# A graph layer on one core: the first three groups fed from six shared edge chunks, and the search for the others by differences of rows

## What is computed

```python
msg = jax.nn.relu(x[src] + edge_attr)
agg = jax.ops.segment_sum(msg, dst, num_segments=50000)
h = x + agg
h = jax.nn.relu(h @ W1 + b1) @ W2 + b2
out = layernorm(x + jax.nn.relu(h), axis=-1)
```

## Time and profile before

| | us |
|---|---|
| median of 3 runs | 477.14 (476.47 to 477.19) |
| the profiled execution | 474.89 |
| its span, first to last instruction | 473.0 |
| PE busy | 457.9 (97%) |
| DVE busy | 434.3 (92%) |
| ACT busy | 395.7 (84%) |
| POOL busy | 365.7 (77%) |

### The profile page before, as it was taken

One profiled execution on the slowest core, in us unless ns is written; L12 is line 12 of the kernel. 1 busy time (PEld: TensorE's weight loads), 2 busy tenths in 40 slices (PEclk: granted clock), 3 DMA queues, 4 the chain that ended last, 5 costly groups with the idle time before them and its releaser, 6 DMA issues.

```text
span 473.0 us, 10533 instructions
## 1 busy us (share of the span) xinstructions
PE 457.9 (97%) x3033; PEld 378.0 (80%) x3033; DVE 434.3 (92%) x1761; ACT 395.7 (84%) x924; POOL 365.7 (77%) x403
## 2 busy tenths in 40 slices
PE   7879999999999999999999999999999999999994
PEld 5657888888888888888888888888888888888883
DVE  5658999999999999999999999999999999999996
ACT  2349888888888989888988888888889898888885
POOL 6546888888877776787888888888888888888843
PEclk9989999999999999999999999999999999999998
DMA  5625666666667676666666666666666666666632
GB/s 131 178 75 174 185 197 192 197 194 196 195 179 208 180 207 182 209 180 195 192 199 191 196 196 193 199 190 196 194 196 190 200 187 202 186 198 188 198 110 87
DMA packets 83613, 86.80 MB, mean 184 GB/s; under 512 B 11767, under 2 KB 79252, under 8 KB 83556
## 3 DMA queue, kind: packets, MB, share of 16 engines
q1 hardware_dynamic: 74388, 68.76, 46.3%
q0 software_dynamic: 8496, 17.38, 14.2%
q10 hardware_dynamic: 672, 0.00, 0.1%
HBM read 60.51 MB, written 25.60 MB: 182 GB/s over the span
## 4 chain that ended last, share of the span: by engine, by line
PE 95%; DVE 1%; another core or an unknown queue 1%; ACT 1%; issue 0%; DMA 0%; DVEq 0%
PE h_ps L930 37%; PE h1T_ps L922 36%; PE hT_ps L886 12%; PE hT_ps L859 9%; PE h1T_ps L413 1%; DMA dst_first<-in_dst_dram 0%; ACT h1T L777 0%; PE prep_ps L423 0%; ACT hT L771 0%; DVE h L632 0%; DVE stats L653 0%; ACT std L782 0%; DVE z L646 0%; PE prep_ps L912 0%
## 5 line engine op out<-in xcount | busy, mean ns | idle before, releaser
L115 POOL DMA_INDIRECT x_src<-in_x_dram,src_of x256 | 269.4, 1052 | 84.8 <-issue 58.0
L930 PE MATMUL h_ps<-w_sb,h1T 128*128 128x128 f32 x1564 | 197.9, 276 | 1.8 <-issue 1.6
L922 PE MATMUL h1T_ps<-hT,w_sb 128*128 128x384 f32 (+1 forms) x524 | 191.6, 488 | 3.7 <-ACT hT L771 3.7
L777 ACT ACTIVATE h1T<-h1T_ps,b_sb 128x384 f32<-128x384 f32 (+1 forms) x262 | 151.7, 580 | 50.7 <-issue 32.7
L930 PEld LDWEIGHTS h_ps<-w_sb,h1T 128*128 128x128 f32 x1564 | 185.5, 192 | 2.6 <-issue 2.1
L922 PEld LDWEIGHTS h1T_ps<-hT,w_sb 128*128 128x128 f32 x524 | 89.9, 192 | 39.0 <-ACT hT L771 3.5
L796 ACT ACTIVATE y<-z,shift,rstd 128x128 f32<-128x128 f32 x261 | 113.6, 482 | 0.6 <-DVE shift L673 0.5
L632 DVE TENSOR_TENSOR h<-h_ps,b_sb 128x384 f32<-128x384 f32 x131 | 72.7, 555 | 25.6 <-PE h_ps L930 14.7
L549 POOL TENSOR_SCALAR y<-z,rstd,shift 128x128 f32<-128x128 f32 x123 | 85.1, 692 | 13.6 <-DVE shift L673 9.1
L653 DVE BATCH_NORM_STATS2 stats<-z 128x6 f32<-128x128 f32 x391 | 88.7, 282 | 0.1
L859 PEld LDWEIGHTS hT_ps<-ident,x_sb 128*128 128x128 f32 (+1 forms) x379 | 49.5, 142 | 39.6 <-issue 22.8
(11 more groups left out here) (133 smaller groups left out, 182.8 us busy)
## 6 DMA issues: line engine op xcount, KB each, us to landing
x_sb<-in_x_dram SPq DMA_DIRECT2D x130, 192.0 KB
out_dram<-y SPq DMA_DIRECT2D x130, 192.0 KB
pre_msg<-in_edge_attr_dram SPq DMA_DIRECT2D x130, 128.0 KB
x_src<-in_x_dram,src_of POOLq DMA_INDIRECT x256
w_sb<-in_w_dram SPq DMA_DIRECT2D x2, 128.0 KB
dst_rows<-in_dst_dram SPq DMA_DIRECT2D x1, 97.7 KB
x_src<-in_x_dram,first_pairs POOLq DMA_INDIRECT x4, 2.7
b_sb<-in_b_dram SPq DMA_DIRECT2D x1, 64.0 KB, 3.1
```

The source lines that it names most:

```text
L115: nc.gpsimd.indirect_dma_start(out=c["x_src"][:, g % EB, k, :], out_offset=None, in_=x, in_offset=bass.IndirectOffsetOnAxis(ap=index, axis ...
L777: nc.scalar.activation(h1T[:, h, 0:n, 0:p], h1T_ps[h][:, 0:n, 0:p], ACT.Relu, bias=b1_sb[:, h:h + 1]).then_inc(h1_ready, 1)
L922: nc.tensor.matmul(h1T_ps[h][:, 0:n, 0:p], w1_sb[:, h * 128:(h + 1) * 128], hT[:, 0:n, 0:p], start=True, stop=True).then_inc(h1_summed, 1)
L930: last = nc.tensor.matmul(h2_ps[g % 2][0:p, t, :], h1T[:, h, t, 0:p], w2_sb[:, h, :], start=(h == 0 and t == 0), stop=(h == HC - 1), skip_ ...
```

## The change

Three things.

1. **Groups 0 to 2 from fixed chunks.** Six chunks of 128 edges (edges 0 to 767) serve the first three groups together. `FIRST_SELS` lists nine pairs of group and chunk, with the range of columns that the pair can reach; a chunk that straddles two groups is multiplied once for each. The search begins at group 3 (`FIRST_ROW = 3`). `msg_whole` is gone: every chunk has a high and a low part.
2. **The search by differences.** Instead of marking the one row that holds a boundary, DVE marks all rows before it (`row_before`), and PE multiplies with `row_steps`, the difference of each row to the row before it, so that the sum telescopes to the wanted row. This drops `dst_next`, `next_of` and `row_holds`, and needs a second copy of the list, moved by one row (`dst_prev`, 99 KB), and one subtraction of 125x200. ACT's conversion of the rows (L403) is gone.
3. **The checks moved** from the first groups to groups 8 to 26 of the steady loop; PE's part (`find_ends`) to group 10. The steps of the search on DVE after the counting are interleaved with the first messages.

The orders of the first groups on all five engines are written anew. Core of the diff:

```diff
-FIRST_ROW = 2
+FIRST_ROW = 3
-TARGETS_FOUND, TARGETS_CHECKED, CHECKED = (12, 16), 20, 30
+ENDS_MARKED, ENDS_FOUND, ENDS_CHECKED = 8, 10, 12
+ORDER_FOUND, ORDER_CHECKED, LIMITS_CHECKED = 14, 16, 18
+TARGETS_FOUND, TARGETS_CHECKED, CHECKED = (20, 22), 26, 30
-FIRST_CHUNKS = 4
-PARTS = {g: [slice(0, 1), slice(1, 2)] for g in range(4)}
+FIRST_GROUPS, FIRST_CHUNKS = 3, 6
+FIRST_SELS = [(0, 0, 0, 128), (0, 1, 56, 128),
+              (1, 1, 0, 92), (1, 2, 0, 128), (1, 3, 72, 128),
+              (2, 2, 0, 56), (2, 3, 0, 128), (2, 4, 16, 128), (2, 5, 88, 128)]
+PARTS = {g: [slice(0, 1), slice(1, 2)] for g in range(FIRST_GROUPS)}
...
# sync
+        start_edge_attr(sp, edge_attr, 2, 2 * K * EW, c)
         sp.wait_ge(c["window_loaded"], 16)
+        start_x(sp, x, 2, 2, c)
...
-        load_ea(2)
-        load_x(2)
         load_ea(3)
         load_x(3)
...
# gpsimd, first part
+        for k in range(2):
+            pool.wait_ge(pairs_loaded[k], 16)
+            start_first_gather(nc, x, k, c)
+        pool.wait_ge(more_pairs_loaded, 16)
+        start_first_gather(nc, x, 2, c)
+        start_first_gather(nc, x, 3, c)
+        pool.wait_ge(start_ready, 1)
+        start_windows(nc, pairs, c)
+        start_first_gather(nc, x, 4, c)
+        start_first_gather(nc, x, 5, c)
...
# vector, search
-        link(dve, nc.vector.tensor_scalar(row_before[:, 0:K, :], node_row[0:ROWS, 0:K, :], first_of[:, 0:1], None, ALU.is_gt))
-        dve.wait_ge(next_loaded, 16)
-        link(dve, nc.vector.tensor_tensor(next_of[:, :], dst_next[:, :], highest[:, :], ALU.max))
...
+        dve.wait_ge(dst_loaded, 16)
+        dve.wait_ge(prev_loaded, 16)
+        dve.wait_ge(prev_cleared, 1)
+        nc.vector.tensor_tensor(row_steps[:, 1:ROW + 1], dst_rows[:, :], dst_prev[:, :], ALU.subtract).then_inc(row_steps_ready, 1)
+        dve.wait_ge(pool_consts, 5)
+        dve.wait_ge(first_dst_ready, 1)
         select_first(nc, 0, c)
         select_first(nc, 1, c)
...
# scalar, loads
+        for k in range(2):
+            act.dma_start(first_pairs[:, k, :], pairs[k * EW:(k + 1) * EW, :]).then_inc(pairs_loaded[k], 16)
+        act.dma_start(dst_prev[1:ROWS, :], dst[0:edges - ROW].rearrange("(r e) -> r e", e=ROW)).then_inc(prev_loaded, 16)
+        act.dma_start(first_pairs[:, 2:FIRST_CHUNKS, :], pairs[2 * EW:FIRST_CHUNKS * EW, :].rearrange("(k p) a -> p k a", p=EW),
...
# vector, first groups
+        checks["count_starts"](dve)
+        checks["first_edges"](dve)
         add_edge_attr(0, 0)
+        checks["split_edges"](dve)
+        dve.wait_ge(c["first_dst_ready"], 2)
+        select_first(nc, 2, c)
+        checks["start_edges"](dve)
+        low_part(0, 0)
         add_edge_attr(0, 1)
+        select_first(nc, 3, c)
+        low_part(0, 1)
         add_edge_attr(1, 0)
+        select_first(nc, 4, c)
         low_part(1, 0)
+        add_edge_attr(1, 1)
+        select_first(nc, 5, c)
+        low_part(1, 1)
+        select_first(nc, 6, c)
+        select_first(nc, 7, c)
+        add_edge_attr(2, 0)
+        select_first(nc, 8, c)
+        low_part(2, 0)
         target_nodes(nc, dve, dst_ps, c).then_inc(targets_ready, 1)
+        add_edge_attr(2, 1)
+        add_bias(0)
+        low_part(2, 1)
         dve.wait_ge(targets_ready, 1)
...
         select(3)
         add_x(0)
         statistics(0)
         aggregate(0)
+        add_edge_attr(3)
         add_bias(1)
+        low_part(3)
...
# scalar, first groups
         high_part(0, 0)
+        high_part(0, 1)
+        copy_hT(0)
+        high_part(1, 0)
+        hidden(0, 0)
+        high_part(1, 1)
         act.wait_ge(c["starts_summed"], 1)
...
+        hidden(0, 1)
+        high_part(2, 0)
+        copy_hT(1)
         source_nodes()
         hidden(1, 0)
+        high_part(2, 1)
         hidden(1, 1)
         copy_hT(2)
         hidden(2, 0)
+        deviation(0)
+        high_part(3)
         hidden(2, 1)
         copy_hT(3)
...
# tensor, first groups
+        sum_first(0, fill=True)
+        checks["keep_busy"](1, 256)
+        sum_first(1, final=True)
+        checks["turn_starts"](pe)
         turn_x(1)
+        sum_first(2)
         pe.wait_ge(c["w1_loaded"], 16 * (1 + HC))
         hidden_sum(0)
+        sum_first(3)
+        pe.wait_ge(c["w2_loaded"], 16)
+        output_sum(0, 0)
+        sum_first(4, final=True)
+        output_sum(0, 1)
         pe.wait_ge(c["starts_row_ready"], 1)
         turn_windows(nc, pe, src_ps, dst_ps, c)
+        hidden_sum(1)
+        turn_x(2)
+        for i in range(5, 8):
+            sum_first(i)
+        output_sum(1, 0)
+        sum_first(8, final=True)
+        output_sum(1, 1)
+        hidden_sum(2)
+        turn_x(3)
+        output_sum(2, 0)
+        sum_messages(3)
+        output_sum(2, 1)
...
+            if g == ENDS_FOUND:
+                checks["find_ends"](pe)
```

More of the change, by code:

```diff
@@ L70, in parts_to @@
     return sum(len(parts(i, c)) for i in range(g))
-def halves_to(g, c):
-    return sum(len(parts(i, c)) - (i in WHOLE) for i in range(g))
 def loads_to(slot, g):
@@ L83, in gathers_to @@
 def gathers_to(slot, g, c):
-    return 16 * sum(windows(i, c) for i in range(slot, g + 1, EB) if i >= 4)
+    return 16 * sum(windows(i, c) for i in range(slot, g + 1, EB) if i >= FIRST_GROUPS)
 def rows(dram, g, c):
@@ L427, in prepare_tensor, with keep_busy, turn_starts @@
                              start=(t == 0), stop=False, skip_group_check=True)
[L428 removed]
+        keep_busy(1, 256)
+    def keep_busy(times, columns):
+        for _ in range(times):
+            nc.tensor.matmul(c["h1T_ps"][0].rearrange("p t n -> p (t n)")[:, 0:columns], ident[:, :],
+                             ident[:, :] if columns == 128 else c["x_sb"][:, 0, 0:2, :].rearrange("p t d -> p (t d)"),
+                             start=True, stop=True)
+    def turn_starts(pe):
         pe.wait_ge(starts_ready, 1)
         nc.tensor.matmul(starts_ps, window_start[:, 0:1], ident[0:R, 0:R], start=True, stop=True).then_inc(starts_summed, 1)
[L431 removed]
     return dict(sync=prepare_sync, gpsimd=prepare_gpsimd, vector=prepare_vector, scalar=prepare_scalar, tensor=prepare_tensor,
[L434 removed]
+                keep_busy=keep_busy, turn_starts=turn_starts, count_starts=count_starts, first_edges=first_edges,
+                split_edges=split_edges, start_edges=start_edges, mark_ends=mark_ends, find_ends=find_ends, check_ends=check_ends,
+                find_order=find_order, check_order=check_order, check_limits=check_limits, find_targets=find_targets,
+                check_targets=check_targets, set_general=set_general, sum_flags=sum_flags)
 def main_path(nc, x, pairs, edge_attr, out, c, sb, sem, checks):
@@ L738, in main_vector @@
                 add_edge_attr(g + 3)
+            if g == ENDS_MARKED:
+                checks["mark_ends"](dve)
+            if g == ENDS_CHECKED:
+                checks["check_ends"](dve)
+            if g == ORDER_FOUND:
+                checks["find_order"](dve)
+            if g == ORDER_CHECKED:
+                checks["check_order"](dve)
+            if g == LIMITS_CHECKED:
+                checks["check_limits"](dve)
             if g in TARGETS_FOUND:
@@ L903, in sum_second @@
[L903 to L914 removed]
+            pe.wait_ge(msg_lo_ready, parts_to(g, c) + 1)
@@ new lines, in sum_messages @@
+            for k in range(windows(g, c)):
+                if g == LAST:
+                    p0, p1, tile = 0, LP, last_sel[:, :]
+                elif g == END:
+                    p0, p1 = (0, WP) if k == 0 else (END_LO, END_LO + END_WP)
+                    tile = end_sel[:, k, :]
+                else:
+                    p0, p1, tile = LO[k], LO[k] + WP, sel[:, g % EB, k, :]
+                cols = tile.rearrange("p (t q) -> p t q", t=n)[:, :, 0:p1 - p0]
+                for part in (msg_hi, msg_lo):
+                    last = nc.tensor.matmul(sum_bank(g)[:, 0:n, p0:p1], part[:, g % EB, k, :], cols,
+                                            start=False, stop=(k == windows(g, c) - 1), skip_group_check=True)
```

313 lines of the change are left out of this document (106 added, 207 removed).

## The result

The change made the kernel slower: 483.99 us (median of 4 runs, 483.25 to 485.17) against 477.16, a ratio of 1.0149 with a 95% interval of 1.0126 to 1.0171. The forecast was 474.5, its range ended at 477.5. The profiled run took 485.17, its span 483.5.

What follows compares the result with a forecast made beforehand. PE, busy 97% of the span, was taken as the bound, so only an earlier start of its series helps. Terms -1.0 - 1.2 - 0.9 + 0 + 0.35 + 0.2 = -2.55: 477.14 - 2.6 = 474.5 us, range 467.5 to 477.5.

Steps and rivals of the forecast that it cites:

- and land at 12.1: Search, at the start: POOL's windows go out at 8.7 and land at 12.1 instead of 11.73, not needed before 14.5.
- The loads: At the start: dst_prev lands at 4.8, PE begins the search 0.2 later, bounds 0.3 earlier to 1.0 later.
- Groups 0 and 1: First two groups: hidden_sum(0) at 11.2 instead of 12.23, -1.0 us; hidden_sum(1) at 15.0 instead of 17.18, -1.2 more.
- Groups 2 and 3: Next two groups: hidden_sum(2) at 18.8, hidden_sum(3) at 22.3 against 25.4 for before without its pause, -0.9 us more.
- with 3.2 us the second is there at 19.9: Group 3's second gather, started at 16.7, takes 3.2 us from issue to use and is there at 19.9.
- The checks in the series: Checks moved into the steady loop: PE's two matmuls in group 10 cost +0.35 us, DVE's pieces +0.2 (0 to 2.6).
- The pause: ACT's waits near 20 to 26 us for PE work long done, priced at 6.5 us; the change leaves it, 0.
- rival 1: At the start: the pause goes with something the new order avoids, gaining 6.5 us more, to 468.0; chance 0.31.
- The clock: PE's clock at the start: busy about 3.9 of 4.6 us from 10.4 to 15.0, so nothing charged.
- rival 2: PE falls to half clock between 9 and 23 us, 2.5 us a group; two groups give 479.5; chance 0.12.
- Rival 3: In the series: DVE can't hide the checks, PE pays 2.6 us instead of 0.2, giving 476.9; chance 0.11.
- The median: Whole run: the runs' median stands 2.25 us above the profiled execution, carried over to the forecast without a reason.

Runs made afterwards that it cites:

- e1: The changed kernel with FIRST_ROW back at 2, so 128 windows are searched and fetched instead of 127: 474.67 us, 0.994 of the kernel before.
- e3: e1 with seven more window gathers in the series, of 128, 127, 126, 120, 112, 64 and 111 rows, into an unread tile: 495.76 us.
- k3: The change with 128 windows, w1 and b1 loaded later, gather lead 3 instead of 4, and iotas spacing POOL's gathers up to group 13: 470.12 us, 0.9898.
- k1_lead_grows: The change with 128 windows, w1 and b1 loaded later, and a gather lead growing from 2 to 3 to 4 groups: 469.72 us, 1.0037.
- k4: The kernel before with gather lead 3 instead of 4 and iotas spacing POOL's gathers up to group 13: 470.87 us, 0.9912.
- g3: The change with 128 windows and w1 and b1 loaded later, with gather lead 3 instead of 4: 470.45 us, 0.988.
- p1: e1 with the gathers of groups 4 and 5 held until the sums of groups 2 and 3 are copied: 479.48 us (one run).

## Why the prediction was wrong, by its steps

**The failed step: "and land at 12.1".** For the windows I took the 3.4 us of the gather of before and looked only at when it would be issued. The change moves `FIRST_ROW` from 2 to 3, and with it the number of rows from 128 to 127, which the text doesn't mention. It was a price row for another shape: the windows land at 25.3, 15 us after their issue. By e1 this is worth 9.3 us, more than all other terms together. By the rule of the Trainium skill (DMA: Bandwidth & Descriptors, "Why a DMA increments its semaphore by 16 and not by 1") one engine carries all 127 packets; an estimate with it, at the 107 ns that e3 shows for one, is 13.6 us, where the trace of after has 11.2 and e3 15.6.

**The loads.** `dst_prev` was taken as 4.8 and used at 6.48, outside my bounds (1.0 later was the upper one). The pairs of chunks 2 to 5 came at 7.34; before, its four chunks' pairs were in use at 5.41. With them the starts are written at 9.86 instead of 8.3, and `window_start_i` at POOL is 10.29 instead of 8.7. The bound was too narrow, since no row had such a load in company.

**Groups 0 and 1.** In k3, the start without window trouble and pause, `hidden_sum(0)` is at 12.32 (forecast 11.2, before 12.23) and `hidden_sum(1)` at 15.99 (forecast 15.0, before 17.18). The order works as walked, everything 1.0 to 1.1 later; PE begins the search at 6.74 in k3, 1.6 later than walked, by the loads. (The new start has one filler of 256 columns fewer than before, not two as the text says; nothing rests on it.) So -1.0 became +0.1, and both groups together gave -1.2 instead of -2.2.

**Groups 2 and 3.** `hidden_sum(2)` is at 20.11 (forecast 18.8), `hidden_sum(3)` at 25.91 (forecast 22.3). The step that failed is "with 3.2 us the second is there at 19.9". In k1_lead_grows, whose gathers have no iota between, the second is issued at 17.83, 1.1 later than forecast, and DVE's addition starts only at 22.86:

```profile
22.86 0.43 DVE L628 TENSOR_TENSOR pre_msg<-pre_msg,x_src 128x256 f32<-128x256 f32 x1 [2.86 <-DMA x_src<-in_x_dram,src_of]
```

That is 5.0 us from issue to use. I had carried over 3.2 from a gather at 5.58. Loads of groups 3 and on and further gathers run beside the later one; that they are the reason wasn't tested. Group 3 waits for its gathers, and -0.9 is lost: k4's `copy_hT(3)`, the old order, is at 25.03, k3's at 25.37.

**The checks in the series.** Right. `find_ends` takes 0.35 in the chain and the step 3.75 instead of 3.41, +0.34 for a forecast of +0.35; DVE's pieces show once, at group 14, as +0.13 for +0.2:

```profile
67.27 0.44 PE hT_ps L903 x4
67.71 0.35 PE prep_ps L369 x2
68.06 1.34 PE h_ps L937 x12
```

**The pause.** Its price of 6.5 us was right for the two groups (k4: 6.5), but too high for the kernel, which got 4.6 of it back in k4. That the change leaves it in was right also. Of the three causes that rival 1 lists it hangs on the first, the gathers in a row; but searching one group less made the row no shorter, for it is POOL's lead that sets it. I counted "six gathers in a row (eight before)"; the trace of after has eight from 27.12 to 36.88.

**The clock.** In after it is full to 18.9 and half from there to 29.1, where the windows had left PE with 1.48 us of work in 10:

```profile
16.00:26.00 10.00, 1.48 (x11) 1.32 (x11) 0.79 (x3) 0.13 (x1) 0.08 (x1) 0.64 0.10 29
26.00:30.00 4.00, 3.88 (x14) 2.27 (x13) 2.09 (x9) 2.20 (x6) 2.27 (x3) 0.61 0.63 167
```

That is rival 2's symptom with another cause: it follows the wait, and it makes `hidden_sum(1)` 1.3 us longer (2.78 against 1.45), a part of the 9.3. In k3, with the same few fillers and no such wait, the clock stays full. As a cause rival 2 is refuted. Rival 3 is refuted by the two steps above.

**The median.** I carried 2.25 us from the profiled run to the median. For after the profiled run was the slowest of its four, 1.2 above the median. The offset was no property of the kernel.

## What stays open

How a row of gathers on POOL holds PE's completions isn't shown, only that the pause follows the row, that 0.7 us of other work between gathers keeps it away, and that the runs on one of the six chips of the experiments are free of it (one batch, so the chip and the moment aren't told apart). Steps of about 5.1 us stand behind most extra gathers of e3, three of them with a "remote" wait of 1.7 to 2.4 us of DVE, though no more than three gathers follow each other there: it may be the same thing. A step of 4 to 4.8 us at group 57, seen in after and several others, has no row and no "remote" wait beside it. I tested neither. The best time measured is k3's or g3's (0.9898 and 0.988 of before, on different chips); the two were not run side by side.

## What to carry to other kernels

Where an edit shifts a constant, write down each shape that hangs on it, and reprice every DMA whose row count changes: the largest divisor up to 16 is what counts. With 1 (127 rows) the gather landed after 19.66 us, with 3 (111 rows) after 6.94, against 3.67 for 128. Padding the row count by one unused row was worth 2% of this kernel.

When an engine waits for work that its producer had long finished, look at what the gathering engine issued without a gap just then, and try a smaller lead or other work between the gathers before rewriting the order of everything. Run the kernel before on more than one chip, for such a wait can be missing on one.

## What was unexpected of the hardware

One indirect gather of 127 rows took POOL 2.60 us and landed after 19.66 us; 128 rows took 0.98 and 3.67. During six to ten indirect gathers at 0.30 us distance, or just after, PE's completion signals come late, by up to 6.7 us (in p1 two of its semaphores rise 5.4 and 6.7 us after the matmuls' ends). And the same kernel, the one before, ran in 468.5 us on one chip and 475.4 to 477.2 on the others, a difference of 6.9 to 8.7 us, somewhat above the 6.5 of the pause.
